# Two small products of an attention kernel: from fp32 to two fp32r products on stacked parts

## The reference, cut to what matters

```python
C_q = Q @ Wq_d                               # 256 x 512 times 512 x 64
C_kv = K @ Wkv_d                             # 1601 x 32
CqWqk = (C_q @ W_qk).reshape(b, n, H, LKV)   # 256 x 64 times 64 x (16 heads * 32)
scores = jnp.einsum('bnhl,bkl->bhnk', CqWqk, C_kv) / sqrt(LKV)
attn = softmax(scores)
out = attn @ (C_kv @ Wv_u)                   # per head
```

## Time and profile before

| | us |
|---|---|
| median of 3 runs | 1947.76 (1945.25 to 1950.1) |
| the profiled execution | 1948.22 |
| its span, first to last instruction | 1946.4 |
| TensorE busy in the span | 1872.9 (96%) |
| stage 1, up to 305 | 305 |
| `before()` of stage 2, in 305 to 345 | 40 |
| rest of stage 2, 345 to 975 | 630 |
| stage 3 | 971 |

### The profile page before, as it was taken

One profiled execution on the slowest core, in us unless ns is written; L12 is line 12 of the kernel. 1 busy time (PEld: TensorE's weight loads), 2 busy tenths in 40 slices (PEclk: granted clock), 3 DMA queues, 4 the chain that ended last, 5 costly groups with the idle time before them and its releaser, 6 DMA issues. The chain is left out here.

```text
span 1946.4 us, 23155 instructions
## 1 busy us (share of the span) xinstructions
PE 1872.9 (96%) x8570; PEld 1337.1 (69%) x8570; DVE 1019.9 (52%) x1852; ACT 904.3 (46%) x1726; POOL 655.7 (34%) x630
## 2 busy tenths in 40 slices
PE   7999997999999999999979999999999999999998
PEld 6999894444465555555577777767777677777764
DVE  3464434667655565665635555554444645554415
ACT  2333331445334344444326666645666456655660
POOL 0000000000000000000017777755777577766770
PEclk9999996899999999999989999999999999999998
DMA  5978863000010111021058444544444355443201
GB/s 182 286 243 268 280 209 113 1 1 18 29 59 27 34 66 33 33 67 44 22 177 197 111 108 118 133 124 116 126 113 112 81 132 135 124 124 98 69 25 44
DMA packets 192950, 208.42 MB, mean 107 GB/s; under 512 B 87425, under 2 KB 157569, under 8 KB 192838
## 3 DMA queue, kind: packets, MB, share of 16 engines
q1 hardware_dynamic: 177124, 188.92, 34.1%
q10 hardware_dynamic: 15714, 18.03, 3.1%
HBM read 128.90 MB, written 77.94 MB: 106 GB/s over the span
## 5 line engine op out<-in xcount | busy, mean ns | idle before, releaser
L1475 POOL TENSOR_TENSOR pl<-pf,ph 128x512 fp32r<-128x512 f32 (+1 forms) x480 | 623.4, 1320 | 258.6 <-ACT pf L1669 258.6
L1666 ACT ACTIVATE ph<-ps 128x512 fp32r<-128x512 f32 (+1 forms) x480 | 288.4, 601 | 361.9 <-PE ps L1562 361.9
L1749 DVE TENSOR_REDUCE pm<-ps 128x1 f32<-128x464 f32 x480 | 307.7, 642 | 249.5 <-PE ps L1493 245.9
L1187 DVE TENSOR_REDUCE pm<-ps 128x1 f32<-128x400 f32 (+3 forms) x544 | 283.1, 572 | 96.9 <-PE ps L1020 84.0
L1080 ACT ACTIVATE pr<-ps 128x512 f32<-128x512 f32 (+1 forms) x416 | 219.1, 601 | 193.9 <-PE ps L952 192.9
L1669 ACT ACTIVATE pf<-ps 128x512 f32<-128x512 f32 (+1 forms) x480 | 289.7, 603 | 0.7 <-POOL pl L1475 0.7
L965 PE MATMUL ps<-pr,cv 128*64 128x512 f32 (+1 forms) x832 | 209.0, 618 | 0.0
L1580 PE MATMUL ps<-ph,vh 128*97 128x512 f32 (+1 forms) x480 | 193.0, 402 | 0.0
L1583 PE MATMUL ps<-pl,vh 128*97 128x512 f32 (+1 forms) x480 | 190.1, 396 | 0.8 <-POOL pl L1475 0.7
L1581 PE MATMUL ps<-ph,vl 128*97 128x512 f32 (+1 forms) x480 | 189.9, 396 | 0.0
L89 POOL TENSOR_SCALAR ln_v<-ln_mv 128x2 f32<-128x2 f32 x9 | 1.9, 214 | 507.1 <-DVE ln_mv L70 507.1
(11 more groups left out here) (273 smaller groups left out, 3098.2 us busy)
## 6 DMA issues: line engine op xcount, KB each, us to landing
woT<-wo_turned SPq DMA_DIRECT2D x30, 768.0 KB, 6.1
v_scr<-vst SPq DMA_DIRECT2D x16, 1152.0 KB
cnat<-in_ctx_dram SPq DMA_DIRECT2D x16, 768.0 KB
q_scr<-qst SPq DMA_DIRECT2D x48, 256.0 KB, 2.5
vh<-v_scr SPq DMA_DIRECT2D x15, 672.0 KB
vl<-v_scr SPq DMA_DIRECT2D x15, 672.0 KB
home<-k_scr SPq DMA_DIRECT2D x14, 696.4 KB, 8.9
k_scr<-home SPq DMA_DIRECT2D x24, 384.0 KB, 7.8
```

The lines of the kernel that those rows point to most:

```text
L1187: dve.reduce_max(pm[:, j, ch:ch + 1], src[:, 0:(cuts if s < S else next_cuts)[ch][1]], AX)\
L1475: pool.tensor_tensor(pl[0:m, n % 2, cols], pf[0:m, half, :], ph[0:m, n % 2, cols].bitcast(F32), ALU.subtract).then_inc(plo, 1)
L1666: act.activation(ph[0:keys[kt], n % 2, cols], src, ACT.Exp, scale=S1).then_inc(phi, 1)
L1749: ins = dve.reduce_max(pm[:, j, ch:ch + 1], at[:, 0:cuts[ch][1]], AX)
```

## The change

The products with W_qk are computed in fp32r from parts. `wqk` now has 128 partitions: the weights' high part (rounded to fp32r) in 0 to 63, the low part in 64 to 127. `cq` also has 128 partitions, with the high part of the latent queries in both halves; `cql` holds their low part in 64 partitions. One product over 128 rows gives (high + low weights) times high queries, a second over 64 rows adds high weights times low queries. So each `a` item has four matmul instructions of one pass in place of two fp32 ones.

For the queries to stand in both halves, `latent_queries` and the item `cq` compute each product twice, once into each half of 64 PSUM partitions. ACT casts 128 rows where it copied 64, and DVE, which did not read this item, subtracts to make `cql` and is now the item's last reader.

The parts of the weights are made once, in stage 1. The weights are loaded six times (three for each half of partitions) into a buffer that the dequantised weights held, at piece 7 in place of three loads at piece 3; the load of the bias moves from piece 2 to piece 7 too. After the keys of piece 9 ACT casts 128 x 1536 elements and DVE subtracts 64 x 1536. Small buffers share memory with others: the loaded `wd` stands in `cn`, the scales and zero points in `bias0`.

```diff
@@ load_small(n), SP, stage 1
-                elif n == 3:
-                    for r in range(3):
-                        sp.dma_start(wqk[:, :, r * HD0:(r + 1) * HD0],
-                                     A["L0_xattn_W_qk"].rearrange("l (h e) -> l h e", e=HD0)).then_inc(w_small, 16)
+                elif n == 7:
+                    sp.wait_ge(w_deq, DC)
                     sp.dma_start(bias0[:, :], A["L0_ffn_bias"].rearrange("(a n) -> a n", a=1).to_broadcast([P, D]))\
                         .then_inc(w_small, 16)
+                    sp.wait_ge(*turned(("w", F_1 - 1)))
+                    for half in range(2):
+                        for r in range(3):
+                            sp.dma_start(wqk_in[half * LQ:(half + 1) * LQ, :, r * HD0:(r + 1) * HD0],
+                                         A["L0_xattn_W_qk"].rearrange("l (h e) -> l h e", e=HD0)).then_inc(w_qk, 16)
@@ latent_queries, PE, stage 1 (the item cq of stage 2 alike)
                 for c in range(DC):
-                    mm = pe.matmul(out[0:LQ, 0:T], wqd[:, c, :], xaT[:, c, :], start=(c == 0), stop=(c == DC - 1))
+                    for half in range(2):
+                        mm = pe.matmul(out[half * LQ:(half + 1) * LQ, 0:T], wqd[:, c, :], xaT[:, c, :],
+                                       start=(c == 0), stop=(c == DC - 1))
@@ ACT and DVE, stage 1, after the keys of piece 9
+                    if g == ("k", 9, 2):
+                        act.wait_ge(w_qk, 16 * 6)
+                        act.copy(wqk[:, :, :], wqk_in).then_inc(wqk_hi, 1)
...
+                if g == ("k", 9, 2):
+                    dve.wait_ge(wqk_hi, 1)
+                    dve.tensor_tensor(wqk[LQ:2 * LQ, :, :], wqk_in[LQ:2 * LQ, :, :], wqk[LQ:2 * LQ, :, :], ALU.subtract)\
+                        .then_inc(wqk_lo, 1)
@@ the item a, PE, stage 2
                     for j in range(2):
-                        mm = pe.matmul(out[0:HD1, j * T:(j + 1) * T], wqk[:, 2 * g[2] + j, :], cq[:, :],
-                                       start=True, stop=True)
+                        pe.matmul(out[0:HD1, j * T:(j + 1) * T], wqk[:, 2 * g[2] + j, :], cq[:, :], start=True, stop=False)
+                        mm = pe.matmul(out[0:HD1, j * T:(j + 1) * T], wqk[0:LQ, 2 * g[2] + j, :], cql[:, :],
+                                       start=False, stop=True)
@@ the item cq, ACT and DVE, stage 2 (stage 1 alike)
-                    act.copy(cq[:, :], src[0:LQ, 0:T]).then_inc(done["act"], 1)
+                    act.copy(cq[:, :], src[:, 0:T]).then_inc(cq_hi, 1)
...
+                elif g[0] == "cq":
+                    dve.wait_ge(cq_hi, g[1])
+                    dve.tensor_tensor(cql[:, :], src[0:LQ, 0:T], cq[0:LQ, :], ALU.subtract).then_inc(done["dve"], 1)
```

More of the change, by code:

```diff
@@ L158, in build @@
             small = {n: early.enter_context(nc.sbuf_tensor(n, shape, F32)) for n, shape in
-                     (("bias0", [P, D]), ("wqd", [P, DC, LQ]), ("wqk", [LQ, H0, 3 * HD0]), ("wvu", [P, NG * 2, 2, HD0 + 1]),
-                      ("cq", [LQ, T]))}
+                     (("bias0", [P, D]), ("wqd", [P, DC, LQ]), ("wvu", [P, NG * 2, 2, HD0 + 1]))}
+            small |= {n: early.enter_context(nc.sbuf_tensor(n, shape, F32R)) for n, shape in
+                      (("wqk", [2 * LQ, H0, 3 * HD0]), ("cq", [2 * LQ, T]), ("cql", [LQ, T]))}
             context_products(nc, A, ident, negid, ps, ln, home, wkvh, wkvl, wqh, wql, w0T, w1T, *small.values(),
@@ L202, in context_products @@
         wrow = sb("wrow", [P, NW, D])
-        wd = sb("wd", [P, DC, HD0])
+        wd = cn[:, 1, :, 0:HD0]
         w0i = sb("w0i", [P, DC, D], I32)
-        w0s = sb("w0s", [P, DC, D // P])
-        w0z = sb("w0z", [P, DC, D // P])
+        w0s, w0z = [bias0[:, i * DC * (D // P):(i + 1) * DC * (D // P)].rearrange("p (o i) -> p o i", o=DC) for i in range(2)]
         w0n = w0i[:, :, :].bitcast(F32)
         xaT = w0n[:, 0:2, :].rearrange("p a (c m) -> p (a c) m", c=2)
+        wqk_in = w0n[:, 0:3, :].rearrange("p a n -> p (a n)").rearrange("p (h e) -> p h e", e=3 * HD0)
         wo_out = sb("wo_out", [HD1, 2, 2, D], F32R)
@@ L253, in last_reader @@
             kind = g[0]
-            if kind in ("x", "cq") or kind == "w" and F_0 <= g[1] < F_1:
+            if kind == "x" or kind == "w" and F_0 <= g[1] < F_1:
                 return "act"
@@ L593, in _ @@
                         act.wait_ge(*turned(g))
+                        act.wait_ge(wqk_lo, 1)
                         act.copy(xaT[:, 2 * g[1]:2 * g[1] + 2, :], bank_of(g).rearrange("p (c m) -> p c m", c=2))\
@@ L675, in group @@
                     c_lo(g[1])
+                elif g[0] == "cq":
+                    dve.wait_ge(cq_hi, 1)
+                    dve.tensor_tensor(cql[:, :], bank_of(g)[0:LQ, 0:T], cq[0:LQ, :], ALU.subtract).then_inc(done["dve"], 1)
+                if g == ("k", 9, 2):
+                    dve.wait_ge(wqk_hi, 1)
+                    dve.tensor_tensor(wqk[LQ:2 * LQ, :, :], wqk_in[LQ:2 * LQ, :, :], wqk[LQ:2 * LQ, :, :], ALU.subtract)\
+                        .then_inc(wqk_lo, 1)
             line = iter([(n, g) for n in range(N + 1) for g in groups(n)])
@@ L833, in last_reader @@
         def last_reader(g):
-            if g[0] in ("xat", "cq") or g[0] == "xt" and g[2:] == (0, 0):
+            if g[0] == "xat" or g[0] == "xt" and g[2:] == (0, 0):
                 return "act"
```

11 lines of the change are left out of this document (6 added, 5 removed).

## The result

The changed kernel took 1941.90 us (median of 17 executions, 1938.03 to 1949.14); the kernel before took 1948.29 on the same chip (17 executions, 1945.25 to 1952.18). The ratio of the two, taken from all the executions, is 0.9977, 95% interval 0.9969 to 0.9986: 0.23% or some 4.5 us faster (the two medians lie 6.4 us apart, the two means 5.3). That is still inside the 0.3% taken as no change, and inside the range, but the median stands at the forecast's own lower bound of 1942, and the forecast was 1948.9, a little above the kernel before. The time moved, and not that way. The profiled execution took 1947.89 us with a span of 1946.1, near the slow end of the 17, so times of parts are compared here and not the two spans.

The account below looks back on a forecast made before the run. TensorE bounds stage 1 and the long part of stage 2; in before() DVE and ACT chain with it. Terms 0 + 0.6 - 0.2 + 0.2 + 0.3 + 0.3 = +1.2 us on 1947.76 gave 1948.9; range 1939 to 1957.

Parts of the forecast that it names:

- The price of a change of form: On TensorE, switching between products with 64 rows or columns and products with more costs 0.19 us at full clock.
- What it costs then: Changed item a in the long part: 0.47 + 4 x 0.19 = 1.23 us, as before; 0 for 21 items, -0.7 to +0.7.
- the three items behind values: Long part, one item in each of batches 1 to 3: an added change, +0.19 us each, +0.6 in all.
- The sum of the long part: Stage 2's long part: 0 for 21 items and +0.6 us for the three that follow values.
- `before()`: Half-clock part of stage 2: -0.5 us over six rounds, +0.3 at the start; sum -0.2, from -1.2 to +0.6.
- The first two items: Start of before(): seven products and seven changes, 4.03 us until ACT's second cast against 3.73, +0.3.
- `cq`: Four cq items, sixteen records each: column halves run at once as eight pairs, +0.2 us taken, +0.4 at most.
- VectorE's wait: At the cq items DVE holds its maxima back behind ACT's cast: +0.3 us taken for all.
- Stage 1: Loads moved to piece 7 and casts at piece 9: ACT's part hidden, DVE's lag covered by the ring; +0.3 us taken.
- the stores' cover: Stage 1: key stores begin at 152.4, land at 159.1, ACT needs the first at 160.14: covered by 1.0 us.
- The first: Rival: changes inside item a cost nothing, only entry and exit; -17.6 us, 1930; chance 0.06 in full.
- its half price: First rival with changes inside item a at half price: -9 us, 1939; chance 0.10.

Follow-up runs that it names:

- mirrored: Changed kernel with the second half's two products of item a in reverse order (128, 64, 64, 128 rows): 1936.47 us, ratio 0.9944.
- fp32 over 128 rows: Against full rows, item a is one fp32 product over all 128 rows, queries unrounded in both halves: 1934.97 us, ratio 0.9937.
- full rows: Changed kernel with low queries in both halves of cql, both products over 128 rows: 1923.99 us, ratio 0.9867; again 1924.92, 0.9886.
- light loads: Two weight loads of 64 rows of 2 KB in place of six: 1945.15 us against the changed kernel, 1928.89 with full rows.
- the kernel with only the other parts: Changed kernel, but item a stays fp32 over 64 rows of the high parts, low parts left out of its sum: 1949.82 us, ratio 0.9997.

## Why the prediction was wrong, point by point

Sums from the records, against the whole. The item with its neighbours is 1.22 us before; 1.17 after, 0.80 mirrored, 0.87 as fp32 over 128 rows, 0.47 with full rows, for 21 items of the long part. The three that follow values are 0.12 dearer in the changed kernel, and there the others save less too. "First part" is the time from stage 2's first `a` to the product of the maxima's row, 35.6 us before, from the profiles:

| kernel | 24 items | first part | sum | whole, by the means |
|---|---|---|---|---|
| after | -0.8 | -1.7 | -2.5 | -5.3, -5.4, -2.5; light loads -3.3 |
| mirrored | -9.3 | -3.0 | -12.3 | -11.5 |
| fp32 over 128 rows | -8.0 | -3.8 | -11.8 | -12.1 |
| full rows | -17.4 | -6.3 | -23.7 | -26.6, -22.1; light loads -20.6 |

Two terms, read from records, account for every kernel within about 3 us. This was the frame of the prediction, and for the three large gains it holds. For the changed kernel itself 3 us is as much as the whole sum: the records carry 2.5 us of a gain of some 4.4 (the mean of the three), and the other 2 are in no step of the sum.

**The price of a change of form is the step that failed**, in "What it costs then". I took 0.19 us, from the maxima's products beside values. The count of four was right. Between two short fp32r records the price is 0.168: a record with a change on both sides takes 0.286, one with none 0.118, one with a change behind it 0.206 and one with a change ahead of it 0.197 (the last two in the mirrored kernel). The rows that I had would have given it, for the item before was 1.03 long with four records of 0.215 in it, 0.86; the 0.17 between them is the late part of one change and the early part of another, one whole price. The item is 1.17, not 1.23, where the old one is 1.22, and 21 items give -1.1, not 0 and outside the -0.7 to +0.7 that I allowed. For the three items behind values (the sixth of each batch, not the fifth) I forecast +0.6; they gave 0.35. The sum of the long part was to be +0.6 and was -0.8.

**`before()`** was to give -0.2 and gave -1.7. Two sizes were off. At half clock a change costs 0.24 us, not 0.27, so ScalarE starts 1.92 after the item and not 1.97. And I counted the round only from the item's start. The kernel before also paid for the change on entry, in the maximum's product ahead of `a`; the changed item has the same form as that product, and the round lost another 0.13 there: 0.27 a round in place of 0.09, in six rounds (0.38 in the first). For the full clock the prediction had that part (its 0.10 ahead of 1.03), in `before()` it forgot it. The first two items came out even (3.74 against 3.73 us), where +0.3 was forecast. Price and entry together make 2.9 of the 5.6 us between the forecast sum of +1.2 and the measured -4.4.

**`cq`**: pairs run at once, +0.0 measured, +0.5 forecast with VectorE's wait. Right in kind.

**Stage 1**: the stores' cover held, with the issue time even shorter than taken (8.59 us, not 11). What followed at 186 to 240 us was not in the sum: about +2, cause open, where +0.3 stood.

**The clock** was not in the sum either. Over all executions the mean granted clock is 0.9686 for the kernel before (109 executions), 0.9712 for the changed kernel (41). Times 1948 and 1944 us that is 61 and 56 us of clock lost; 0.9 of the 5 is the shorter first part. The profiles show the rest as a fall of 3.4 us more or less at the same few places: in the rest of stage 2 and stage 3 together 71.6 to 79.5 us at half clock in four profiles of the kernel before, 62.6 to 72.1 in four of the changed one (light loads among them). The means are 75.7 and 67.8, so 8 us less at half clock, which costs 4 us less. The four of the kernel before are 76.7, 71.6, 79.5 and 75.2, so two profiles of one kernel can differ by as much. Stage 3, which the change doesn't touch, took 917.3 us in the mean of those four profiles of the changed kernel and 919.6 in the four of the kernel before, from its first product to the end. In these eight profiles the parts add up: stage 1 +2.5, the first part -1.7, the rest of stage 2 -0.7, stage 3 -2.3, together some -2 us. The other 2 us of the 4.4 no profile shows. Why falls become shorter hundreds of us behind the change stays open, and the kernel with only the other parts has 0.9701 with no gain at all, so the clock by itself settles nothing.

**The rivals.** The first, that changes inside an item are free, would have had records 0.12 apart; they are 0.29 apart. It was its half price that lay nearest, at 1939, but by chance: the price is nine tenths and not half, and the records carry only 2.5 us. The forecast rested on a cancellation, 0.56 us saved and 0.56 paid back in each item. An error of a tenth in the price is then already the whole answer of the long part, 1.1 us. The Trainium skill (TensorEngine Tiling (Array Packing), Key Properties) has TensorE drain on a change of tiling mode. The runs agree in that each change has a price, 0.168 us at full clock and 0.24 at half; that it is a drain which is paid, no run shows.

## What to carry to other kernels

- On TensorE count changes of form as you count products. With records of 256 columns one change costs more than one fp32r product (0.168 against 0.118 us). Filling 64 rows up to 128, even with terms that the result hardly needs, took the item from 1.17 to 0.47 us and the kernel from 1944 to 1924; merely ordering equal forms side by side took it to 1936.
- Before splitting fp32 into parts, try the wide form by itself: fp32 over 128 rows gave half of the whole gain, 2.7 us of it through a clock that rose early.
- A record's distance to the next start can be too short as its cost: compare the records behind it with their like as well. The fp32 item over 128 rows reads as 0.68 us to the next start and costs 0.87.
- Where a forecast is a difference of two like sums, take each price from the records of the very form, and count entry and exit in every stretch in the same way.

## What the runs showed of the hardware that was not expected

- The scores behind the fp32 item over 128 rows start 0.68 us after the item's start, though its four records cost 0.87: the rest shows in the scores' own records, as the 0.65 us of the pair in place of 0.46.
- Over the stretch from 312 to 340 us the kernel with fp32 over 128 rows had a granted clock of 0.68, and the one with fp32r over full rows 0.50. The view by stretch of the first (columns as above):

```profile
312.00:340.00 28.00, 23.60 (x62) 13.91 (x60) 18.57 (x35) 4.66 (x8) 4.00 (x4) 0.68 0.44 116
```

  The clock of fp32's rose to full at 330 us, 24 us after it had fallen and 14 us ahead of the end of the first part; it was at half again from 343.4 to 350.2 us. All others stayed at half for 41 to 48 us, until 6 to 9 us behind the end of their first part. Why this one rose early is open. The mean clock of its six executions is 0.978 against 0.974 with full rows. It was still slower, since its items are longer.
- SP's issue of 1024 runs of 128 B took 1.4 us each in the mean of six (8.59), and two transfers of 64 rows of 2 KB took 2.04 together, with no effect on the end: the cheaper issue was worth nothing here.
